# Scatters and padding transfers one per slot, and causal masks of several heads in one matmul ahead of the scores

## The reference

```python
x = x + attn_a(layernorm(x), w_qkv, w_proj)      # causal, 16 heads of 16
x = x + ffn(layernorm(x), ...)                   # attention, then 4 experts of 256 -> 1024 -> 256
x = x + attn_b(layernorm(x), ...)                # attention over the 8 sequences at each position
x = x + ffn(layernorm(x), ...)

# attn_a, for each head
attn = einsum('bhqd,bhkd->bhqk', q, k) * scale
attn = where(causal, attn, -inf)                 # key after query: masked
a = clip(attn, -100, 100); e = exp(a - max(a)); p = e / (sum(e) + 1e-6) + 1e-8; p = p / sum(p)
out = einsum('bhqk,bhkd->bhqd', p, v)

# ffn, after its attention and first layernorm
expert_idx = remainder(floor(x @ router_w + router_b), 4)
ff_out = sum over e of where(expert_idx == e, relu(x @ W1[e] + b1[e]) @ W2[e] + b2[e], 0)
return layernorm(x + ff_out)
```

## Time and profile before

| | |
|---|---|
| median of 3 runs | 2610.97 us (2608.83 to 2614.83) |
| profiled execution | 2617.94 us, span 2616.2 us, mean granted clock 0.97 |
| TensorE busy | 2440.0 us, 93% of the span, 15044 matmuls |
| VectorE busy | 1836.5 us, 70% |
| ScalarE busy | 1439.2 us, 55% |
| GpSimd busy | 1350.9 us, 52% |
| DMA | 305.91 MB, mean 117 GB/s |

### The profile page before, as it was taken

The page is one execution under the profiler, slowest core; times in us unless marked ns, Lnnn a source line. Parts: engine busy times, 40 slices in busy tenths (PEclk is TensorE's granted clock), DMA queues, the critical chain, the costliest instruction groups (busy, mean ns, idle before and its releaser), DMA issues. The chain is left out here.

```text
span 2616.2 us, 46472 instructions
## 1 busy us (share of the span) xinstructions
PE 2440.0 (93%) x15044; PEld 1418.3 (54%) x15044; DVE 1836.5 (70%) x3685; ACT 1439.2 (55%) x2991; POOL 1350.9 (52%) x1358
## 2 busy tenths in 40 slices
PE   6999999999999999989899699987999999989998
PEld 3555555554444444349799366653344444358897
DVE  4989998999778888844343558867778888844333
ACT  3666666666777777653233223214777777653332
POOL 5356665563234545445555569843334445435555
PEclk8999999999999999999999789988999999999999
DMA  5333333333434444234555200015434444245554
GB/s 159 100 100 108 105 102 105 111 99 101 118 110 132 130 128 124 84 114 166 199 181 174 70 1 17 17 54 138 119 110 128 129 129 125 72 134 168 182 196 139
DMA packets 249938, 305.91 MB, mean 117 GB/s; under 512 B 28034, under 2 KB 224865, under 8 KB 249700
## 3 DMA queue, kind: packets, MB, share of 16 engines
q1 hardware_dynamic: 238164, 275.37, 35.2%
q0 software_dynamic: 10176, 26.27, 2.8%
q10 hardware_dynamic: 1360, 1.31, 0.2%
HBM read 210.32 MB, written 92.84 MB: 116 GB/s over the span
## 5 line engine op out<-in xcount | busy, mean ns | idle before, releaser
L769 DVE TENSOR_REDUCE neg_max_af<-sc_af 128x1 f32<-128x512 f32 (+3 forms) x864 | 551.8, 665 | 111.7 <-PE sc_af L474 85.1
L690 ACT ACTIVATE prob_af<-sct_af 128x512 f32<-128x512 f32 (+1 forms) x864 | 484.9, 582 | 250.5 <-PE sct_af L495 138.1
L769 DVE TENSOR_REDUCE neg_max_f<-sc_f 128x1 f32<-128x512 f32 x512 | 334.2, 685 | 92.4 <-PE sc_f L474 89.6
L690 ACT ACTIVATE prob_f<-sct_f 128x512 f32<-128x512 f32 x512 | 291.3, 598 | 137.0 <-PE sct_f L495 134.8
L474 PE MATMUL sc_af<-stack_k_af,stack_q_af 96*128 96x512 bf16 (+3 forms) x1024 | 331.9, 344 | 18.4 <-DVE neg_max_af L769 13.6
L495 PE MATMUL sct_af<-stack_q_af,stack_k_af 99*128 99x512 bf16 (+3 forms) x1024 | 331.5, 346 | 6.3 <-ACT prob_af L690 4.9
L1599 PE MATMUL y_ps_e<-w_r,hT_e 128*128 x1120 | 258.6, 384 | 8.8 <-issue 5.0
L798 DVE SCALAR_TENSOR_TENSOR prob_af<-prob_af,w_r 128x512 f32<-128x512 f32 (+2 forms) x224 | 231.9, 1043 | 25.9 <-ACT prob_af L690 25.7
L526 PE MATMUL out_af<-prob_af,v_aug_af 128*32 128x512 f32 (+3 forms) x2048 | 232.3, 525 | 6.8 <-DVE prob_af L798 5.9
L1599 PEld LDWEIGHTS y_ps_e<-w_r,hT_e 128*128 128x128 f32 x1120 | 209.6, 192 | 39.8 <-issue 13.3
L495 PEld LDWEIGHTS sct_af<-stack_q_af,stack_k_af 99*128 99x128 bf16 x1024 | 100.1, 98 | 229.8 <-ACT prob_af L690 147.7
(11 more groups left out here) (382 smaller groups left out, 4732.3 us busy)
## 6 DMA issues: line engine op xcount, KB each, us to landing
w_r<-in_f_W_dram SPq DMA_DIRECT2D x66, 1024.0 KB, 6.4
stack_k_af<-k_parts_d SPq DMA_DIRECT2D x64, 384.0 KB, 4.2
k_parts_d<-parts_af SPq DMA_DIRECT2D x187, 128.0 KB
q_parts_d<-parts_af SPq DMA_DIRECT2D x96, 128.0 KB
stack_q_af<-q_parts_d SPq DMA_DIRECT2D x64, 192.0 KB, 3.0
stack_k_f<-k_parts_d SPq DMA_DIRECT2D x32, 384.0 KB, 4.3
w_next<-in_f_W_dram SPq DMA_DIRECT2D x12, 1024.0 KB
k_parts_d<-parts_f SPq DMA_DIRECT2D x91, 128.0 KB
```

What stands on the lines that cost most here:

```text
L690: nc.scalar.activation(dst, src.rearrange("p (h q) -> p h q", h=len(heads)), ACT.Exp).then_inc(S.exp_done, 1)
L769: nc.vector.tensor_reduce(M.neg_max[:, qt, heads[0]:heads[-1] + 1], src, AX.X, ALU.max, negate=True).then_inc(S.max_done, 1)
```

## The change

Experts: `scatter` of the last sequence is split into `find_places`, the five small steps, in slot 6, and `scatter_tile`, one transfer each in slots 7 to 10. `write_padding` is split into `find_padding` in slot 11 and `pad_expert`, one transfer each in slots 12 to 15. Every one of them stands at the end of its slot, behind `gather_prev`. `scatter` itself, still used for the sequence before the last, calls the parts in one go.

Causal layer: the masks of all heads in a unit are written by one matmul, which comes ahead of the scores and starts the accumulation; its moving operand is the mask repeated for each head, and its output the diagonal blocks of the heads. The scores are then added to it. Columns outside the diagonal blocks are first written by the scores.

```diff
--- before.py
+++ after.py
@@ -469,13 +469,15 @@
                     pe.wait_ge(S.max_done, u - 2)
                 bank = M.sc[u % 3]
                 cols = P * (qt + 1) if causal(n) else T
+                masked = causal(n)
+                if masked:
+                    diagonal = bank[:, 0:len(heads) * cols].rearrange("p (h k) -> p h k", h=len(heads))[:, :, qt * P:qt * P + P]
+                    nc.tensor.matmul(diagonal, C.ident_bf[:, :], C.mask_qk[:, :].unsqueeze(1).to_broadcast([P, len(heads), P]),
+                                     start=True, stop=True)
                 for at, h in enumerate(heads):
                     o = at * cols
                     last = nc.tensor.matmul(bank[:, o:o + cols], M.stack_q[0:96, g, h, qt * P:qt * P + P], M.stack_k[0:96, g, h, 0:cols],
-                                            start=True, stop=True)
-                    if causal(n):
-                        last = nc.tensor.matmul(bank[:, o + qt * P:o + qt * P + P], C.ident_bf[:, :], C.mask_qk[:, :],
-                                                start=False, stop=True, skip_group_check=True)
+                                            start=not masked, stop=True, skip_group_check=masked)
                 last.then_inc(S.sc_ps, 1)
 
             def score_t(n, g, kt, i):
@@ -490,13 +492,15 @@
                     pe.wait_ge(S.exp_done, u - 1)
                 bank = M.sct[u % 2]
                 q0 = kt * P if causal(n) else 0
+                masked = causal(n)
+                if masked:
+                    diagonal = bank[:, 0:len(heads) * (T - q0)].rearrange("p (h q) -> p h q", h=len(heads))[:, :, 0:P]
+                    nc.tensor.matmul(diagonal, C.ident_bf[:, :], C.mask_kq[:, :].unsqueeze(1).to_broadcast([P, len(heads), P]),
+                                     start=True, stop=True)
                 for at, h in enumerate(heads):
                     o = at * (T - q0)
                     last = nc.tensor.matmul(bank[:, o:o + T - q0], M.stack_k[0:99, g, h, kt * P:kt * P + P], M.stack_q[0:99, g, h, q0:T],
-                                            start=True, stop=True)
-                    if causal(n):
-                        last = nc.tensor.matmul(bank[:, o:o + P], C.ident_bf[:, :], C.mask_kq[:, :],
-                                                start=False, stop=True, skip_group_check=True)
+                                            start=not masked, stop=True, skip_group_check=masked)
                 last.then_inc(S.t_ps, 1)
 
             def floor_row(n, g, i):
@@ -1875,7 +1879,12 @@
 
             def scatter(i):
 
-                b = i % NB
+                find_places(i)
+                for t in range(KT):
+                    scatter_tile(i, t)
+
+            def find_places(i):
+
                 pool.wait_ge(S.rank_sb, i + 1)
                 pool.wait_ge(S.counted, i + 1)
                 pool.wait_ge(S.scattered, 16 * KT * i)
@@ -1885,26 +1894,31 @@
                 link(nc.gpsimd.tensor_tensor(R.half[:, :, :], R.own[:, :, 0:2], R.own[:, :, 2:4], ALU.add))
                 link(nc.gpsimd.tensor_tensor(R.pos[:, :], R.half[:, :, 0], R.half[:, :, 1], ALU.add))
                 nc.gpsimd.tensor_copy(R.pos_i[:, :], R.pos[:, :]).then_inc(S.placed, 1)
-                pool.wait_ge(S.placed, i + 1)
-                pool.wait_ge(S.x1_ready, i + 1)
-                pool.wait_ge(S.numbered, i + 1)
-                for t in range(KT):
-                    pool.indirect_dma_start(R.sorted_x, bass.IndirectOffsetOnAxis(ap=R.pos_i[:, t:t + 1], axis=0),
-                                            R.x_out[b % 2][:, t, :], None).then_inc(S.scattered, 16)
+
+            def scatter_tile(i, t):
+
+                if t == 0:
+                    pool.wait_ge(S.placed, i + 1)
+                    pool.wait_ge(S.x1_ready, i + 1)
+                    pool.wait_ge(S.numbered, i + 1)
+                pool.indirect_dma_start(R.sorted_x, bass.IndirectOffsetOnAxis(ap=R.pos_i[:, t:t + 1], axis=0),
+                                        R.x_out[(i % NB) % 2][:, t, :], None).then_inc(S.scattered, 16)
 
             def number_last():
 
                 pool.wait_ge(S.x1_normed, i_last + 1)
                 pool.iota(R.x_out[b_last % 2][:, :, D].bitcast(I32), pattern=[[P, KT]], base=T * b_last, channel_multiplier=1).then_inc(S.numbered, 1)
 
-            def write_padding():
+            def find_padding():
 
                 for e in range(NE):
                     link(nc.gpsimd.tensor_tensor(R.pad_at[:, e:e + 1], C.pad_base[:, e:e + 1], R.rank[:, KT * NE + e:KT * NE + e + 1], ALU.add))
                 link(nc.gpsimd.tensor_copy(R.pad_i[:, :], R.pad_at[:, :]))
-                for e in range(NE):
-                    pool.indirect_dma_start(R.sorted_x, bass.IndirectOffsetOnAxis(ap=R.pad_i[:, e:e + 1], axis=0),
-                                            C.pad[:, :], None).then_inc(S.route_padded, 16)
+
+            def pad_expert(e):
+
+                pool.indirect_dma_start(R.sorted_x, bass.IndirectOffsetOnAxis(ap=R.pad_i[:, e:e + 1], axis=0),
+                                        C.pad[:, :], None).then_inc(S.route_padded, 16)
 
             def gather_prev(s):
                 i = s % 2
@@ -1954,9 +1968,13 @@
                 if s == 1:
                     number_last()
                 if s == 6:
-                    scatter(i_last)
-                if s == 7:
-                    write_padding()
+                    find_places(i_last)
+                if 7 <= s < 7 + KT:
+                    scatter_tile(i_last, s - 7)
+                if s == 7 + KT:
+                    find_padding()
+                if 8 + KT <= s < 8 + KT + NE:
+                    pad_expert(s - 8 - KT)
                 if L and s == 9:
                     pool.memset(L.half[:, :], -0.5)
                     pool.memset(L.ones3[:, :], 1.0)
```

## The result

The changed kernel takes 2587.86 us, median of 5 runs (2582.32 to 2597.39), against 2610.97 (2608.14 to 2614.83) for the kernel before: ratio 0.9917, 95% interval 0.9895 to 0.9938. That is 23.1 us less, where 21.4 less was forecast.

A forecast was written before the change was run, and what follows sets the result against it. TensorE was taken as nearest its limit in the causal sequences; in the experts stages only its waits counted. Terms -9.5 - 10.9 - 1.0 = -21.4 us, from a median of 2611.0, gave 2589.6, range 2582 to 2604.

The forecast's parts named there:

- Second experts stage, -9.5: Second experts stage: all seven late tile starts return to the 7.25 us beat, gaining 9.5 us.
- The chain store, row load, transpose: Experts stages: a late GpSimd store delays SyncE's row load and so TensorE's transpose; 3.45 us, then 2.3 more.
- waits for `rstd_e`: Second experts stage: VectorE's waits for this GpSimd result, 23.4 us in five pieces, would vanish.
- The add stays 2.95 us behind its gather: Second experts stage: GpSimd's add keeps this distance from its gather even with a scatter between them.
- First experts stage, -10.9: First experts stage: of 12.9 us lost, all but 2 are regained, 10.9 us; bounds 6 and 12.9.
- one or two tiles are late, near the loads of the next layer: First experts stage: at most this many tiles would stay late after the change.
- first stage held by its own loads: Rival, first experts stage: next-layer weights and small loads delay stores and gathers regardless of GpSimd; gain 16.5, 2594.5 us, chance 0.20.
- Masks, -1.0 with bounds -2 and 0: Causal layer: 320 fewer mask matmuls save 2.1 us at most, half perhaps lost waiting for VectorE; 1 us gained.
- completion moves little: Causal layer: in a one-head unit, scores started one mask later end when the mask after the scores did.
- matmuls' fixed part: Causal layer: merging saves only each removed mask matmul's fixed cost, 6.6 ns each, 2.1 us at most for 320.
- Cover: Experts stages: GpSimd's 1.90 us idle wait for the gather hides one 1.23 us transfer per slot.
- Its rival, 0.58 us over the beat per slot: Experts stages: idle time isn't free, slots take 7.83 us; 1.9 us lost per stage, up to 4; chance 0.15.

The follow-up runs named there:

- next_loads_later: The changed kernel with the next layer's loads and their preparation six slots later in the first experts stage; 2594.42 us, ratio 0.9922 to the kernel before.
- masks_merged_behind: The kernel before with masks merged but left behind the scores, experts part unchanged; 2598.27 us against 2611.74, causal stage 543.9 us.
- transfers_ahead_of_gather: The changed kernel with each scatter and padding transfer ahead of the slot's gather instead of behind it; 2585.33 us.
- experts_only: The kernel before with only the scatter and padding part of the change, masks as before; 2600.24 us, ratio 0.9952.
- masks_only: The kernel before with only the mask part of the change, experts part as before; 2598.88 us, ratio 0.9940.

## Why the prediction came out right, and by what errors

The total was right (21.4 forecast, 23.1 measured), the terms were not.

1. *Second experts stage, -9.5.* Right in mechanism, too large: 7.5 in its seven tiles, 5.5 over the stage. The chain store, row load, transpose was the one that held, and the waits for `rstd_e` fell by three quarters; they did not vanish, as the prediction had it. "The add stays 2.95 us behind its gather" failed in five of the eight slots with a transfer (3.3 to 5.2 us), because the gather itself lands later there.
2. *First experts stage, -10.9.* Mis-sized: about 4.8. The step that failed is "one or two tiles are late, near the loads of the next layer": all five tiles are late, and next_loads_later shows that those loads and their preparation are most of the reason. This was the rival "first stage held by its own loads", which took 6 for it. Part of the error was the sample: before's profile, with 13.0 us lost, was the worst of six, whose mean is 11.0.
3. *Masks, -1.0 with bounds -2 and 0.* Mis-sized by far: 8.8 us in the causal stage, 15.7 (10 to 21) by timing. The step that failed is "completion moves little". Whether the signal moved was not measured, and it was beside the point: what moved was the matmul next to an fp32 weight load, 50 ns a pair (47 pairs in seven sequences, so 2.6 us of the stage). The bounds held only the matmuls' fixed part, and not what a changed neighbour does to the instruction behind it. Some 5 us go with the time at the lower clock, 24 us before and 10 after, four stretches fewer at 1.2 us each; the last 1.4 us is about what masks_merged_behind has for the matmuls saved. So the term itself, priced at 1.0 for the matmuls saved, was nearly right, and the two larger ones beside it were missing.
4. *Cover.* The rows at 2386.64 and 2415.73 show slots in which the transfer costs nothing. Its rival, 0.58 us over the beat per slot, did occur in transfers_ahead_of_gather as a slot of 7.94 us, but cost too little to be seen in the stage. That the cover matters for the time is therefore not shown.

That the total came out within 2 us of the forecast is luck: 20.4 us were forecast for the experts part, whose two stages gain 9.9, and 1.0 for the masks, whose stage gains 8.8, and the timings have 3 to 5 us more that no changed stage shows.

Apart, the two parts sum to 28 us, together they give 21.7 to 23.5; the intervals are wide enough for both to be the same.

Left open: why fewer stretches at the lower clock come with masks ahead. In before there are five, each some 25 us behind the first `floor_row` of its sequence, and in experts_only, with the same masks, four; the nine kernels with masks ahead in `sct` have one each, or none. Whether the shorter beat or the denser stream of matmuls does it was not tried, so that these 5 us are the change's is argued from the count over profiles, not from a cause. Nor is it shown whether masks_only gains the 6.9 us that its timing has and its causal stage doesn't.

## What to carry to other kernels

On an engine that is 97% busy, price an edit of the order by its neighbours too: look at what stands just ahead of each pair of fp32 matmuls, and try a long bf16 matmul there in place of a short one or of one with few rows. Spread transfers over the slots, and if you count on a slot's idle time to hide them, take that idle time from several profiles: here it differed from slot to slot, with the time since the last large load was issued. And when a total comes out right, time the parts apart: here an error of some 10 us and one of some 8 cancelled.

## What the runs showed of the hardware

- Indirect gathers of 128 rows took longer to land when they began soon after a 1 MB load was issued. Over both experts stages of the seven kernels with one transfer per slot, from slot 1 on, from gather to add: 159 gathers that began 1.5 to 2.5 us after the load, median 4.24 us (3.03 to 7.54, a tenth above 5.2); 227 that began 3.0 us after it or later, median 2.95 (a tenth above 3.5). In the slots without a scatter or padding transfer it is the same, 4.24 and 2.94, so these are not the reason. That is read from the traces alone; no run moved only the load.
- Against a score of 384 columns, a matmul with 3 rows (`floor_row`) ahead of an fp32 pair costs 100 ns and a 128-column one 50, as the 54 and 47 pairs of before in seven causal sequences show. Behind a score of 512 columns most pairs lose nothing, but in after 7 of 14 L413 ones lose 65 ns.
- A merged mask of 256 columns in two runs, with a repeated operand, takes 112 ns from start to start in the median of 111 in after, a score of 256 columns the same.
